# Four narrow adjacency products at a time in four column groups, and eight strips kept from layer to layer

## The reference

```
h = jnp.maximum(_layernorm(x, axis=-1), 0.0)
x = x + _L2_gnn_ref(h, edge_index, edge_weight, w0, b0, w1, b1, w2, b2, w3, b3)

def _gcn_conv(x, src, dst, norm, w, b, n):      # norm = dinv[src] * w * dinv[dst], self loops of weight 2
    h = x @ w
    msg = norm[:, None] * h[src]
    return jax.ops.segment_sum(msg, dst, num_segments=n) + b
for i, (w, b) in enumerate(ws):
    x = _gcn_conv(x, src, dst, norm, w, b, n)
    if i < len(ws) - 1:
        x = jax.nn.relu(x)
```

## Time and profile before

| | us |
|---|---|
| median of 3 runs | 10391.05 |
| range of the runs | 10386.8 to 10393.5 |
| span of the profiled execution, first to last instruction | 10386.0 |
| c0, the products with strips | 7699.5 to 7833.8 |
| c1, the same | 7871.0 to 8005.7 |
| c3, the same | 8191.6 to 8325.9 |
| the four convolutions with all around them | 7668.6 to 8336.4 |

### The profile page before, as it was taken

One profiled execution on the slowest core, in us unless ns is written; L12 is line 12 of the kernel. 1 busy time (PEld: TensorE's weight loads), 2 busy tenths in 40 slices (PEclk: granted clock), 3 DMA queues, 4 the chain that ended last, 5 costly groups with the idle time before them and its releaser, 6 DMA issues. The chain is left out here.

```text
span 10386.0 us, 121636 instructions
## 1 busy us (share of the span) xinstructions
PE 6161.5 (59%) x33600; PEld 4039.5 (39%) x33601; DVE 6112.8 (59%) x12781; ACT 1635.9 (16%) x2872; POOL 4395.4 (42%) x4142
## 2 busy tenths in 40 slices
PE   4433333144456777761111499984469967777799
PEld 2333332034455444440000255543434345555555
DVE  6666663143346777772000399999950056666798
ACT  0111110000012444330000022213400011222100
POOL 0577775456653666656777400000000055565300
PEclk9999997555557898885555699998999955555599
DMA  2222223111112222230000011112235611111000
GB/s 79 46 54 52 52 53 78 32 43 32 34 40 58 64 66 66 62 62 12 4 4 5 16 43 43 43 34 76 105 156 230 253 24 25 25 25 25 15 0 1
DMA packets 491139, 554.08 MB, mean 53 GB/s; under 512 B 259701, under 2 KB 390093, under 8 KB 477394
## 3 DMA queue, kind: packets, MB, share of 16 engines
q1 hardware_dynamic: 347558, 485.94, 14.3%
q0 software_dynamic: 132160, 43.97, 4.7%
q10 hardware_dynamic: 11232, 21.73, 0.8%
HBM read 454.32 MB, written 95.99 MB: 53 GB/s over the span
## 5 line engine op out<-in xcount | busy, mean ns | idle before, releaser
L1236 POOL DMA_INDIRECT sh_ring<-node,sh_idx x832 | 853.4, 1026 | 1879.2 <-DVE sh_idx L1841 1648.7
L1236 POOL DMA_INDIRECT mx_ring<-node,mx_idx x832 | 890.0, 1070 | 710.7 <-DVE mx_idx L1310 466.0
L421 POOL DMA_INDIRECT slots<-rank_staged,rank_row_i x800 | 952.3, 1190 | 398.6 <-issue 227.7
L1591 PE MATMUL sm_sums<-sm_both,sm_hot 128*128 128x512 f32 x1664 | 842.8, 631 | 468.3 <-issue 468.0
L898 POOL DMA_INDIRECT mid_ring<-typed,mid_idx x832 | 834.6, 1003 | 512.6 <-issue 245.5
L1481 POOL DMA_INDIRECT slots<-sm_rec,sm_row x832 | 859.5, 1033 | 335.6 <-issue 280.4
L401 PE MATMUL rank_found<-rank_next_sb,rank_hot_hi_t 25*125 25x128 f32 x1600 | 407.3, 431 | 824.5 <-ACT rank_next_sb L386 787.0
L401 PEld LDWEIGHTS rank_found<-rank_next_sb,rank_hot_hi_t 25*125 25x125 f32 x1600 | 353.6, 321 | 874.5 <-DVE rank_hot_hi_t L340 843.1
L1578 PE MATMUL sm_net_a<-top,sm_hot_t 128*128 x2496 | 361.6, 283 | 514.2 <-issue 486.9
L1103 PE MATMUL mid_sums<-mid_ring,mid_hot_d 128*128 128x17 f32 x1664 | 392.2, 347 | 356.0 <-issue 325.1
L1512 DVE TENSOR_TENSOR sm_both<-sm_net_m,sm_both 128x512 f32<-128x512 f32 x416 | 300.5, 722 | 477.0 <-issue 445.4
(11 more groups left out here) (393 smaller groups left out, 12803.8 us busy)
## 6 DMA issues: line engine op xcount, KB each, us to landing
strips<-near SPq DMA_DIRECT2D x100, 1600.0 KB, 9.1
mx_far<-far_row SPq DMA_DIRECT2D x208, 256.0 KB
rank_key_row<-key_rows SPq DMA_DIRECT2D x200, 244.1 KB
near<-adj_whole SPq DMA_DIRECT2D x175, 256.0 KB, 2.0
sm_low<-low_row SPq DMA_DIRECT2D x208, 128.0 KB
sh_low<-low_row SPq DMA_DIRECT2D x104, 256.0 KB
feat_t<-mid_out ACTq DMA_DIRECT2D x104, 204.0 KB
mx_feat<-feat_t SPq DMA_DIRECT2D x208, 102.0 KB
```

Of the source, the lines that this page charges most:

```text
L421: pool.indirect_dma_start(m.slots, bass.IndirectOffsetOnAxis(ap=row_i[:, h, j:j + 1], axis=0), staged[:, h, j, :], None).then_inc(sent[h], 16)
L1236: pool.indirect_dma_start(ring[:, h, j, :], None, table, bass.IndirectOffsetOnAxis(ap=idx[:, h, j:j + 1], axis=0)).then_inc(part, 16)
L1591: last = nc.tensor.matmul(sums[r % 2][:, :], hot[:, h, 2 * (r % 2) + j, :], both[:, r % 2, j].rearrange("q a c -> q (a c)"), start=j == 0, ...
```

## The change

Four things change.

1. In the narrow layers (c0 and c3), `g` is taken 32 columns wide (16 features and 16 zeros), the sums have 128 partitions, and strip p of a group of four goes into partitions 32j to 32j + 31 with j = p % 4. The loop goes over columns outside and over the four strips inside, so that neighbouring matmuls write to different groups of 32 partitions. The four partial sums are added later: by d0, whose weights w0 now stand four times at partitions 0, 32, 64 and 96, and in the closing stage by `fold`, four identities above each other, in place of the transposes.
2. Layers 1 and 3 go through the strips from the last to the first. The last eight strips of a layer are the first eight of the next and stay where they are; `strip_plan` lists strip, buffer, count and whether to load. A layer after the first loads 17 strips, and none in the `project` stages.
3. `node_factors` loads the first eight strips ahead of `dinv_row`, and no longer waits for `dinv_row`; c0 waits for it ahead of its scaling.
4. The tables that `adjacency` reads, `table` and `marks`, are 16 bits wide in place of 32. Three more small weight loads are made in `weights`.

```diff
-                for k in range(4):
+                for j in range(4):
+                    load(m.conv_w[0][32 * j:32 * j + D, :], a["L2_gnn_w0"])
+                for k in range(1, 4):
                     load(m.conv_w[k][:, :], a[f"L2_gnn_w{k}"])
+                for k in range(3):
                     load(m.conv_b[k][:, :], a[f"L2_gnn_b{k}"][:, None])
+                load(m.conv_b[3][0:D, :], a["L2_gnn_b3"][:, None])
...
+def strip_plan():
+
+    slots, filled, plan = [], [0] * RING, []
+    for layer in range(4):
+        order = list(range(NB)) if layer % 2 == 0 else list(range(NB - 1, -1, -1))
+        held = [slots[NB - 1 - p] for p in range(RING)] if layer else list(range(RING))
+        slots = [held[p % RING] for p in range(NB)]
+        for p in range(NB):
+            loads = layer == 0 or p >= RING
+            filled[slots[p]] += loads
+            plan.append((order[p], slots[p], filled[slots[p]], loads))
+    return plan
...
 def load_strip(nc, m, sp, k):
 
+    s, slot, _, loads = m.plan[k]
+    if not loads:
+        return
     if k >= RING:
         sp.wait_ge(m.strip_used, k - RING + 1)
-    sp.dma_start(m.strips[:, k % RING, :], m.near[k % NB, :, 0:NP]).then_inc(m.strip_in[k % RING], 16)
+    sp.dma_start(m.strips[:, slot, :], m.near[s, :, 0:NP]).then_inc(m.strip_in[slot], 16)
...
+            if narrow:
+                for b in range(NB):
+                    j, c = b % 4, b * P
+                    nc.tensor.matmul(sums[32 * j:32 * j + 32, c:c + P], m.g[:, b, 0:32], m.twice[:, :], start=opens(c, j), stop=False,
+                                     skip_group_check=True)
+                for p in range(0, NB, 4):
+                    now = steps[p:p + 4]
+                    for s, slot, count, _ in now:
+                        pe.wait_ge(m.strip_in[slot], 16 * count)
+                    for c in range(0, NP, 512):
+                        w = min(512, NP - c)
+                        for j, (s, slot, _, _) in enumerate(now):
+                            last = nc.tensor.matmul(sums[32 * j:32 * j + 32, c:c + w], m.g[:, s, 0:32], m.strips[:, slot, c:c + w],
+                                                    start=opens(c, j), stop=p + 4 + j >= NB, skip_group_check=True)
+                            if c + w == NP:
+                                last.then_inc(m.strip_used, 1)
...
-                last = nc.tensor.matmul(out[:, c:c + w], m.conv_w[k][:, :], m.agg[0:D, c:c + w], start=True, stop=True)
+                last = nc.tensor.matmul(out[:, c:c + w], m.conv_w[k][:, :], m.agg[:, c:c + w], start=True, stop=True)
...
+            if width == D:
+                nc.vector.memset(m.g[:, :, D:32], 0.0)
...
-        @block.sync
-        def _(sp):
-            for s in range(RING):
-                load_strip(nc, m, sp, NB * k + s)
...
-                last = nc.tensor.transpose(out[:, b * D:(b + 1) * D], m.hidden[0:D, b * P:(b + 1) * P], m.ident[0:D, 0:D])
+                last = nc.tensor.matmul(out[:, b * D:(b + 1) * D], m.hidden[:, b * P:(b + 1) * P], m.fold[:, :], start=True, stop=True,
+                                        skip_group_check=True)
...
+            for p in range(RING):
+                load_strip(nc, m, sp, p)
             sp.wait_ge(saved, 16)
-            sp.dma_start(m.dinv_row[:, :], m.dinv_dram[None, :].to_broadcast([P, NP])).then_inc(loaded, 16)
-            for s in range(RING):
-                load_strip(nc, m, sp, s)
-            sp.wait_ge(scaled, 2)
-            sp.wait_ge(loaded, 16)
+            sp.dma_start(m.dinv_row[:, :], m.dinv_dram[None, :].to_broadcast([P, NP])).then_inc(m.row_in, 16)
...
-            m.table, m.marks = rb("table", [1, NT2, 2], I32), rb("marks", [1, NB, 8], I32)
+            m.table, m.marks = rb("table", [1, NT2, 2], U16), rb("marks", [1, NB, 8], U16)
```

More of the change, by code:

```diff
@@ L10 @@
 I32 = mybir.dt.int32
+U16 = mybir.dt.uint16
 BF16 = mybir.dt.bfloat16
@@ L437, in _ @@
         def _(dve):
-            for t in (m.gru_i, m.gru_h, m.mlp2):
+            for t in (m.gru_i, m.gru_h, m.mlp2, m.conv_w[0], m.conv_b[3]):
                 nc.vector.memset(t[tuple(slice(None) for _ in t.shape)], 0.0).then_inc(zeroed, 1)
@@ L1635, in convolve @@
 def convolve(nc, m, stage, layer, width):
+    narrow = width == D
     with ExitStack() as ctx:
         sb, ps, sem = makers(nc, ctx, stage)
-        sums = ps("sums", [width, NP])
+        sums = ps("sums", [P, NP])
         made, done = sem("made"), sem("done")
         block = ctx.enter_context(nc.Block())
+        steps = m.plan[NB * layer:NB * (layer + 1)]
         @block.sync
         def _(sp):
-            for s in range(RING, NB):
-                load_strip(nc, m, sp, NB * layer + s)
+            for p in range(RING, NB):
+                load_strip(nc, m, sp, NB * layer + p)
         @block.vector
@@ L1650, in _ @@
             dve.wait_ge(made, 1)
-            nc.vector.tensor_tensor(m.agg[0:width, :], sums[:, :], m.dinv_row[0:width, :], ALU.mult).then_inc(done, 1)
+            if layer == 0:
+                dve.wait_ge(m.row_in, 16)
+            nc.vector.tensor_tensor(m.agg[:, :], sums[:, :], m.dinv_row[:, :], ALU.mult).then_inc(done, 1)
         @block.tensor
         def _(pe):
-            for b in range(NB):
-                nc.tensor.matmul(sums[:, b * P:(b + 1) * P], m.g[:, b, 0:width], m.twice[:, :], start=b % 4 == 0, stop=False,
-                                 skip_group_check=True)
@@ L1658, in _ @@
-            for s in range(NB):
-                k = NB * layer + s
-                pe.wait_ge(m.strip_in[k % RING], 16 * (k // RING + 1))
-                for c in range(0, NP, 512):
-                    w = min(512, NP - c)
-                    last = nc.tensor.matmul(sums[:, c:c + w], m.g[:, s, 0:width], m.strips[:, k % RING, c:c + w], start=False,
-                                            stop=s == NB - 1, skip_group_check=True)
-                last.then_inc(m.strip_used, 1)
+            opened = set()
@@ new lines, in opens @@
+            def opens(c, j):
+                new = (c // 512, j) not in opened
+                opened.add((c // 512, j))
+                return new
+            if narrow:
[14 more added lines that the diff above has]
+                                last.then_inc(m.strip_used, 1)
+            else:
+                for b in range(NB):
+                    nc.tensor.matmul(sums[:, b * P:(b + 1) * P], m.g[:, b, :], m.twice[:, :], start=b % 4 == 0, stop=False,
+                                     skip_group_check=True)
+                for p, (s, slot, count, _) in enumerate(steps):
+                    pe.wait_ge(m.strip_in[slot], 16 * count)
+                    for c in range(0, NP, 512):
+                        w = min(512, NP - c)
+                        last = nc.tensor.matmul(sums[:, c:c + w], m.g[:, s, :], m.strips[:, slot, c:c + w], start=False,
+                                                stop=p == NB - 1, skip_group_check=True)
+                    last.then_inc(m.strip_used, 1)
@@ L1734, in _ @@
         def _(act):
-            nc.scalar.activation(m.hidden[0:D, :], m.agg[0:D, :], ACT.Identity, bias=m.conv_b[3][:, 0:1]).then_inc(ready, 1)
+            nc.scalar.activation(m.hidden[:, :], m.agg[:, :], ACT.Identity, bias=m.conv_b[3][:, 0:1]).then_inc(ready, 1)
         @block.tensor
@@ L2148, in build @@
         m.gru_i, m.gru_h = sb("gru_i", [D + 1, 4 * D]), sb("gru_h", [D + 1, 4 * D])
-        shapes = [(D, P), (P, P), (P, P), (P, D)]
+        shapes = [(P, P), (P, P), (P, P), (P, D)]
         m.conv_w = [sb(f"conv_w{k}", list(s)) for k, s in enumerate(shapes)]
-        m.conv_b = [sb(f"conv_b{k}", [s[1], 1]) for k, s in enumerate(shapes)]
+        m.conv_b = [sb(f"conv_b{k}", [P, 1]) for k in range(4)]
         m.mlp1, m.mlp_b1, m.mlp2, m.mlp_b2 = sb("mlp1", [2 * D, P]), sb("mlp_b1", [P, 1]), sb("mlp2", [P, 2 * D]), sb("mlp_b2", [P, 2 * D])
```

15 lines of the change are left out of this document (11 added, 4 removed).

## The result

| | before | after |
|---|---|---|
| median of 4 runs each, us | 10388.92 (10378.13 to 10393.5) | 10738.35 (10729.44 to 10744.5) |
| ratio, with its 95% interval | 1 | 1.0336 (1.0322 to 1.0351) |
| span of the profiled execution, us | 10386.0 | 10731.2 |

What follows compares the result with a forecast made beforehand. PE was taken to bound c0 and c3 (5.37 us a strip against 3.85 for DMA). Terms -41 - 41 - 4 + 8 + 1.3 = -76.7 took the median 10391.05 to 10314, range 10288 to 10350.

Steps and rivals of the forecast that it cites:

- The step that failed: In `adjacency`: reading the 16-bit tables is hidden behind PE's 279.4 us wait for DVE's products; 0 us.
- c0, 41 less (34 if the strips begin at 7684.5): First narrow layer: strips begin at 7677, transfers become the bound, products end at 7792.6 instead of 7833.8; 41 us less.
- c3, 41 less: Second narrow layer: eight strips in place, transfers resume after the first round, end at 8284.4 instead of 8325.9; 41 us less.
- all four at once: Rival for c0 and c3: four strips' products run together, a round takes 5.4 us, kernel 10298; chance 0.18.
- Two at a time: Main case for c0 and c3: a strip's second pass runs beside the next strip's first, 10.7 us a round; chance 0.62.
- none at once: Rival for c0 and c3: no products overlap, a round stays at 21.5 us, kernel 10391, no change; chance 0.10.
- exposed loads: Rival for c0 and c3: each record pays its weight load, a round takes 27.7 us, kernel 10468; chance 0.06.
- half clock: Rival for c0 and c3: gaps before rounds keep the clock at 0.50, rounds 21.5 us, kernel 10401; chance 0.04.
- c1 and c2, 0: Wide layers: PE needs 5.37 us a strip and is never short of one, so 24 saved transfers gain nothing; 0 us.
- d0 and p1, 4 less: Stages after c0: with 128 rows d0's last third runs at double speed and p1 may start warm; 4 us less (0 to 6).
- Close, +8: Closing stage: 50 records in 10.8 us, as in p3, replace 25 transposes that took 2.8 us; 8 us more.
- Three more weight loads, +1.3: On the path of `weights`: loads of 0.3 to 0.4 us each on SP, with two memsets; 1.3 us more.

Runs made afterwards that it cites:

- Experiment 12: Changed kernel, 16-bit tables, but PE loads nine values a turn instead of sixteen, in two loads, and waits once; 8572.75 us, ratio 1.0110 to the kernel before.

## Why the prediction was wrong

**The step that failed** is this one: "The 16-bit tables are read by PE and ACT in `adjacency`, where PE waits 279.4 us for DVE's products, so a somewhat cheaper or dearer read is hidden; if it took over 1.6 us longer a turn (279.4 over 176 turns) it would show. **0.**" It has two faults.
- The size. The read was called "somewhat cheaper or dearer" without its row, though the trace of before had it: 1106 ns, 176 times. And it was given no bound from above. The real price is +2.94 us a turn (4.11 - 1.17). A load of a new width, not seen in the trace, should have been bounded from above as well.
- The cover. The 1.6 us were the idle time of the array, and the sequencer spent 1.17 us of them on this very load. What was free was 3.30 - (1.17 + 1.65) = 0.48 us, with the 1.65 of the changed kernel. The trace of before had this number too: at its wait for the DVE's products (L673) PE's sequencer stands 0.58 us a turn on average until its next instruction, and 0.11 in the turns in which it has nothing to wait for; the 0.47 between them was free. (In the changed kernel the average at this place, L678, is 0.12.) A load twice as dear as the row's 1.11 us would already have shown. Experiment 12 is the test: its load is 1.29 us dearer, under 1.6, and its turn grew by 1.02 (0.48 free would leave 0.81).

Since 2.94 is above either threshold the sign follows from the first fault alone: 176 x (2.94 - 1.59) is some 240 us, still more than the convolutions give back. The measured 434 needs the second fault as well: 176 x (2.94 - 0.48) = 433, which is no test, because the 1.65 was taken from the same turn; the 0.47 read from the trace of before gives 435 without it.

Of the other steps, in the order of the prediction (that the sum of the convolutions came out at -84 against -78 is in part luck: c0 gave 7 us less than forecast and c3 13 more):
- **c0, 41 less (34 if the strips begin at 7684.5):** 165.4 became 131.5 us from the issue of `dinv_dram` to the last product, 33.9 less. Two errors met: the strips reached full rate 19 us after the request, not 8; and the tail, 13.03 us for the last 70 records, was shorter than the 17.8 forecast, because four run at once. In it the low clock cost 2.2 us (13.03 less 5.45 for the round and 5.37 for strip 24), where the prediction took 1.7, from a stretch at half speed that it did not work out from a row.
- **c3, 41 less:** 142.2 became 88.0 us from the first write of `g` on, 54.2 less. This is the rival "all four at once", which by its sum had -52: both rounds on kept strips went by in 10.9 us.
- **Two at a time** as the likeliest speed fell. The argument was that "the queue keeps the order of matmuls", and that a product's second pass therefore stands between it and its neighbour. At the start of a round in c0 the records of the first passes of four products begin within 20 ns of each other. The rivals below it (none at once, exposed loads) fall too: weight loads are hidden at 0.10 us a record. Of the half clock something is true: the clock falls in each gap, 0.71 on average in c0, and up to the last round it costs nothing, because the DMA is the bound, as the prediction had it.
- The Trainium skill, "TensorE: Matmul & The Clock Gate" (Part 3), states that matmuls start and end in the order of the program, and that a load overlaps a matmul only if its row group differs. By the second rule each record here would show its load; the trace disagrees. (The same Part also lets a load run ahead into a background weight buffer; no record tells whether that is what happens here.) What the queue's order is among the passes of one float32 product no record shows. The page's 2.38 times for three tiles is below what four give here, 21.5 / 5.45 = 3.9 times. The Trainium skill, "TensorEngine Tiling (Array Packing)", Theoretical Speedup, has up to four, and the trace agrees with that.
- **c1 and c2, 0:** 134.50 us each, as before. Right; of the 24 transfers that the prediction names here, 16 belong to c1 and c2 and 8 to c3.
- **d0 and p1, 4 less:** 4.2 less from c0's last product to c1's first product with a strip. The size is right; 3.7 of it is d0, which took 7.3 us in place of 11.0 at a clock of 0.79, more than the forecast's last third at double speed gives.
- **Close, +8:** 50 records in 10.85 us; the stage took 8.0 more. Right.
- **Three more weight loads, +1.3:** the first load from `table` starts at 7078.9 in both. Not seen.
- **The slices:** the prediction looked at 30 to 33 and called them full clock; 33 reads 5 in the earlier trace rows. `adjacency`, in 28 to 30, where the fourth item of the change acts, is outside the slices it named.

## What to carry to other kernels

An edit that is priced at nothing because an engine waits needs two numbers: the duration of the edited instruction from its own row, and how much of the engine's idle time its sequencer already fills with that instruction. A narrower type is no cheaper by itself: here registers are loaded far faster from 32-bit values than from 16-bit ones, and only as many should be loaded as are needed. When an engine becomes four times as fast the bound can move to the transfers, as it did here, and then the start of the first transfer (tiny writes ahead of it) and the moment at which buffers come free are worth more than the arithmetic.

## What the runs showed of the hardware

- Loading registers from a table in SBUF took 1.11 us for 16 values of 32 bits and 0.55 for 8 (0.07 us a value), but 4.09 for 16 values of 16 bits, 1.93 to 2.14 for 8 and 0.29 for one (about 0.26 a value), on PE's queue as on ScalarE's. Why is open: the runs exclude the packing, not more, and width was not separated from sign (U16 against I32). The Trainium skill, "DMA: Bandwidth & Descriptors" (Latency and other measured facts), gives `tensor_load` a floor of some 600 ns, without saying from which memory; the 293 ns of experiment 12, from SBUF, are below it.
- Four float32 products with 32 columns of weights each ran at once at full speed: 109 records, which take 0.43 us each one after the other, went by in 10.90 us. With neighbours in the same group the same products took 4.4 us a strip in place of 1.4.
- 3200 writes of 4 bytes held transfers of 1600 KB on the same queue down to 31 GB/s for 19 us. On another queue they let them pass (368 GB/s), alternating with them packet by packet, and took 41.1 us to land, for 12.5 KB.
- The clock had fallen to 0.50 within the wait of 13 us ahead of c3's third round (window 8600 to 8607 us), averaged 0.70 in a wait of 8 us in c0 (8147 to 8154.8), and was 0.59 over a stage in which the PE was busy 465 of 1022 us; the same products on the same data took 294 ns in place of 219.
